# A four-part transformer kernel on one core: the order of all its jobs laid out anew, and the value products of two or three attention steps issued as one job

## The reference

```python
x = x + L0_attn(layernorm(x))      # one head, key and value width 64, causal, biases
x = x + L0_ffn(layernorm(x))       # fp8-quantized x @ weight.T + bias, 256 -> 256
x = x + L1_attn(layernorm(x))      # 16 heads of width 16, rotary embedding, causal
x = x + L1_ffn(layernorm(x))       # mixes with the row before, three 256x256 products

# L1_attn, the part that the change touches most
Q, K, V = (proj(W_Q), proj(W_K), proj(W_V))          # each [B, 16, S, 16]
Q = _apply_rope(Q, cos, sin); K = _apply_rope(K, cos, sin)
scores = jnp.einsum('bhsd,bhtd->bhst', Q, K) / jnp.sqrt(jnp.float32(D_K))
scores = jnp.where(causal[None, None], scores, -jnp.inf)
attn = jax.nn.softmax(scores, axis=-1)
out = jnp.einsum('bhst,bhtd->bhsd', attn, V)
out = out.transpose(0, 2, 1, 3).reshape(B, S, D_MODEL)
return jnp.einsum('bsd,ed->bse', out, W_O)
```

## Time and profile before

| what | value |
|---|---|
| median of 3 runs | 2517.73 us (2509.86 to 2520.37) |
| profiled execution, first to last instruction | 2514.1 us |
| PE / DVE / ACT / POOL busy | 2320.8 / 1985.3 / 1512.4 / 525.7 us |
| PE busy share | 92% |
| mean granted TensorE clock | 0.981 |

### The profile page before, as it was taken

One profiled execution on the slowest core, in us unless ns is written; L12 is line 12 of the kernel. 1 busy time (PEld: TensorE's weight loads), 2 busy tenths in 40 slices (PEclk: granted clock), 3 DMA queues, 4 the chain that ended last, 5 costly groups with the idle time before them and its releaser, 6 DMA issues.

```text
span 2514.1 us, 52353 instructions
## 1 busy us (share of the span) xinstructions
PE 2320.8 (92%) x19371; PEld 1053.0 (42%) x19371; DVE 1985.3 (79%) x4326; ACT 1512.4 (60%) x2753; POOL 525.7 (21%) x526
## 2 busy tenths in 40 slices
PE   8889899999999899998999999999999999999998
PEld 4544333333434335353444534344344434332345
DVE  5778689887787887879787787997788688899932
ACT  2234456575655666676675666657566577677762
POOL 5453210302215012120403303031121400000011
PEclk9899999999999999999999999999999999999999
DMA  2322220120211312021121302112021121110111
GB/s 56 83 72 73 76 58 25 38 59 18 83 34 35 82 43 73 15 79 29 42 65 37 91 19 76 40 35 78 12 76 35 42 70 45 31 42 27 28 37 36
DMA packets 185896, 125.41 MB, mean 50 GB/s; under 512 B 84912, under 2 KB 185392, under 8 KB 185648
## 3 DMA queue, kind: packets, MB, share of 16 engines
q1 hardware_dynamic: 184880, 121.16, 17.4%
q10 hardware_dynamic: 768, 0.92, 0.1%
HBM read 62.20 MB, written 59.24 MB: 48 GB/s over the span
## 4 chain that ended last, share of the span: by engine, by line
PE 55%; DVE 29%; ACT 6%; issue 4%; DMA 2%; SPq 2%; DVEq 1%; POOL 1%; POOLq 0%; ACTq 0%
DVE mx L1543 20%; PE psum L1867 12%; PE psum L1845 6%; PE psum L1812 6%; PE psum L1778 4%; ACT probs L1303 4%; PE psum L1742 3%; PE psum L1887 2%; PE psum L1713 2%; PE psum L1898 2%; PE psum L1651 2%; PE psum L1918 2%; PE psum L1799 2%; PE psum L1906 2%; DVE stats L1402 1%
## 5 line engine op out<-in xcount | busy, mean ns | idle before, releaser
L1303 ACT ACTIVATE probs<-psum 128x512 f32<-128x512 f32 x2176 | 1139.4, 607 | 465.8 <-PE psum L1845 310.2
L1543 DVE TENSOR_REDUCE mx<-psum 128x1 f32<-128x512 f32 (+2 forms) x2304 | 1283.4, 620 | 140.9 <-PE psum L1812 99.5
L1867 PE MATMUL psum<-probs,vs 128*17 128x512 f32 (+3 forms) x5120 | 590.7, 543 | 0.7 <-ACT probs L1303 0.3
L1812 PE MATMUL psum<-kst,qst 48*128 48x512 f16 (+3 forms) x2560 | 439.6, 354 | 71.0 <-DVE mx L1543 37.7
L1845 PE MATMUL psum<-qst,kst 50*128 50x512 f16 (+3 forms) x2560 | 428.7, 353 | 55.7 <-DVE mx L1543 19.5
L1812 PEld LDWEIGHTS psum<-kst,qst 48*128 48x128 f16 x2560 | 134.0, 94 | 397.5 <-DVE mx L1543 154.5
L1845 PEld LDWEIGHTS psum<-qst,kst 50*128 50x128 f16 x2560 | 128.2, 94 | 360.1 <-ACT probs L1303 131.4
L1867 PEld LDWEIGHTS psum<-probs,vs 128*17 128x17 f32 x5120 | 93.1, 96 | 155.5 <-issue 127.6
L1088 POOL TENSOR_SCALAR vare<-mv 128x4 f32<-128x4 f32 x64 | 15.5, 241 | 595.5 <-DVE mv L1405 595.5
L1819 PE MATMUL psum<-maskq,identh 64*128 64x128 bf16 (+1 forms) x2048 | 131.1, 205 | 0.0
L1117 POOL TENSOR_TENSOR sums<-probs 128x512 f32<-128x512 f32 x12 | 15.3, 1272 | 494.3 <-ACT probs L1257 494.3
(11 more groups left out here) (173 smaller groups left out, 2876.2 us busy)
## 6 DMA issues: line engine op xcount, KB each, us to landing
qk_dram<-parts SPq DMA_DIRECT2D x168, 128.0 KB
qst<-qk_dram SPq DMA_DIRECT2D x128, 96.0 KB, 2.3
kst<-qk_dram SPq DMA_DIRECT2D x128, 96.0 KB, 2.3
v_dram<-vst SPq DMA_DIRECT2D x64, 136.0 KB, 4.0
vs<-v_dram SPq DMA_DIRECT2D x64, 136.0 KB, 2.1
xs<-x_in SPq DMA_DIRECT2D x16, 512.0 KB, 3.5
x_dram<-xs SPq DMA_DIRECT2D x16, 512.0 KB, 2.9
att_dram<-ast SPq DMA_DIRECT2D x64, 128.0 KB, 2.0
```

The lines of the kernel that those rows point to most:

```text
L1303: act.activation(dst, src, ACT.Exp, scale=DK1 ** -0.5 / LIFT ** 2).then_inc(S["exp"], 1)
L1543: ins = dve.tensor_reduce(mx1[:, n % 2, 2 * g + odd, tile % TPC, c:c + 1], bank(src, at, at + cols), AX.X, ALU.max)
L1812: ins = pe.matmul(two[odd][:, at:at + cols], qst[rows, qslot, pair, P * (tile % TPC):P * (tile % TPC + 1)], kst[rows, kslot, pair, 0:cols] ...
L1867: ins = pe.matmul(bank(7, off, CH, rows=VW, row=32 * h), vtile[:, h, :], probs[:, HG * (step_no(b, hg, k) % PSTEPS) + h, at:at + CH - off] ...
```

## The change

Three things change; the arithmetic does not.

1. **`values` jobs.** Off the diagonal the products of two consecutive steps are one job, on the diagonal those of all three (`group_of`, `group_steps`). Such a job waits for all exponentials of its steps, and whoever waits for a step's values waits for the whole group's. There are 256 `values` jobs where there were 576, with the same 2560 matmuls of the program.
2. **The planner's numbers.** `HOP` is now one number per waiting engine and counts only between engines, `SWITCH` and several durations and landing times are other numbers, and a mode change that falls into a hole costs nothing.
3. **The planner's choice.** A stretch is 2.5 long instead of 40. What its rule is (how much staying in the mode counts, how much a pile of work before DVE or ACT holds back `max` and `scores`, and a weight for each kind on every engine) isn't tried out but drawn from a number in the table `RULES`, two characters a stretch.

Two `values` jobs have become one, and the `max` and `scores` jobs that stood between them stand on its two sides. The diff, cut to its core:

```diff
+def group_of(k):
+
+    q, kbs = STEPS[k]
+    return k - kbs[0] % 2 if kbs[0] < TPC * q else STEP_AT[q, TPC * q]
+
+
+def group_steps(k):
+
+    q, kbs = STEPS[k]
+    return range(k, k + 2) if kbs[0] < TPC * q else range(k, final_step(q) + 1)
+
+
+def valued(step):
+
+    return ("values", step and (*step[:2], group_of(step[2])))
...
-HOP = 0.25
-SWITCH = {("F", "R"): 0.31, ("F", "C"): 0.31, ("R", "F"): 0.15, ("R", "C"): 0.15, ("C", "F"): 0.14, ("C", "R"): 0.14,
...
-STICK = 100.0
+HOP = {"PE": 0.325, "DVE": 0.13, "ACT": 0.14, "POOL": 0.12, "SP": 0.1}
+SWITCH = {("F", "R"): 0.11, ("F", "C"): 0.10, ("R", "F"): 0.18, ("R", "C"): 0.10, ("C", "F"): 0.16, ("C", "R"): 0.08,
...
-STRETCH, WAYS, MOVE = 40.0, 8, 10.0
+STRETCH = 2.5
...
+        for at in range(len(RULES) // 2):
+            if state.todo:
+                rule = base * DIGITS.index(RULES[2 * at]) + DIGITS.index(RULES[2 * at + 1])
+                self.go(state, then, number, (at + 1) * STRETCH, self.rule(rule))
...
+    "!}!}!}!}!}!b%I!U,C!},U('$=*9!}!}!}!}!}!}!}!}!}!}!u+M!}!}$E!}!}!}!})^!u&j&r,A!n!e$1(n!u!I!(%Q$j$z"
...
+CAP = 3.0
+MOVES = (5.0, 20.0, 50.0, 120.0)
...
+    def rule(self, n):
+
+        if n == 0:
+            return 100.0, {"max": 50.0, "scores": 50.0}, {}
+        draw = np.random.RandomState(n)
+        share = draw.uniform(0, 1, 4)
+        move = MOVES[n % 4]
+        by = draw.uniform(-move, move, len(self.kinds))
+        return 150 * share[0], {"max": 100 * share[1], "scores": 100 * share[2]}, dict(zip(self.kinds, by))
...
+                load = {x: min(CAP, max(0.0, free_at[x] - now) + sum(jobs[name][2] for name in ready[x]))
+                        for x in ("DVE", "ACT", "POOL")} if e == "PE" else {}
...
-                    rank = (jobs[name][1] - (STICK if jobs[name][7] == mode and e == "PE" else 0.0) + weights.get(name[0], 0.0),
-                            number[name])
+                    rank = jobs[name][1] - (stick if jobs[name][7] == mode and e == "PE" else 0.0) + weights.get(name[0], 0.0)
+                    if e == "PE" and name[0] in press:
+                        rank += press[name[0]] * load[self.emptied[name[0]]]
+                    rank = (rank, number[name])
...
-                        ("scores", (b, hg, k, j)), ("values", two), lat=0.1, free=(("scores", (b, hg, k, j)), odd))
...
+                        ("scores", (b, hg, k, j)), valued(two), free=(("scores", (b, hg, k, j)), odd))
+            group += sum(CH - span(q, kb) for kb in kbs) / CH
+            if k == group_steps(group_of(k))[-1]:
+                n = group_of(k)
+                add("PE", "values", (b, hg, n), key + 5, 0.055 + 0.853 * group, *exps,
...
-                    wt.job("values", step_before(b, hg, k, PSTEPS))
+                    wt.job(*valued(step_before(b, hg, k, PSTEPS)))
...
-                    b, hg, k = item
-                    q, kbs = STEPS[k]
-                    for j in range(len(score_jobs(k))):
-                        for odd in range(2):
-                            wt.job("exp", (b, hg, k, j, odd))
-                    v_loaded(wt, b, hg, kbs[0] // TPC)
...
+                    b, hg, first = item
+                    for k in group_steps(first):
+                        q, kbs = STEPS[k]
+                        for j in range(len(score_jobs(k))):
+                            for odd in range(2):
+                                wt.job("exp", (b, hg, k, j, odd))
+                        v_loaded(wt, b, hg, kbs[0] // TPC)
```

More of the change, by code:

```diff
@@ L267, in run, with go @@
         state = State(left, self.listed, jobs)
[L268 to L281, removed]
+        self.kinds = sorted({name[0] for name in self.listed})
+        self.emptied = {}
+        for name in self.listed:
+            free = jobs[name][6]
+            if free:
+                self.emptied[(free[0] if free[0] in jobs else free)[0]] = jobs[name][0]
+        base = len(DIGITS)
+        for at in range(len(RULES) // 2):
+            if state.todo:
+                rule = base * DIGITS.index(RULES[2 * at]) + DIGITS.index(RULES[2 * at + 1])
+                self.go(state, then, number, (at + 1) * STRETCH, self.rule(rule))
+        assert not state.todo
         self.home, self.tenants, self.total, self.start = state.home, state.tenants, max(state.free_at.values()), state.start
         return state.order
[L285 to L293, removed]
+    def rule(self, n):
[6 more added lines that the diff above has]
+        return 150 * share[0], {"max": 100 * share[1], "scores": 100 * share[2]}, dict(zip(self.kinds, by))
+    def go(self, state, then, number, until, rule):
         jobs = self.jobs
@@ L353, in go @@
                 if e == "PE" and md != mode:
-                    time += SWITCH.get((mode, md), 0.0)
+                    time += max(0.0, SWITCH.get((mode, md), 0.0) - (now - free_at[e]))
                     mode = md
@@ L477, in chunk_jobs @@
         there = parts_before(b, q, bl)
-        add("PE", "RT", (*c, bl), key(), 0.43, ("RT", p and (*p, bl)), *[("roped", (*c, t)) for t in range(TPC)], ("put", there), lat=0.1,
+        add("PE", "RT", (*c, bl), key(), 0.43, ("RT", p and (*p, bl)), *[("roped", (*c, t)) for t in range(TPC)], ("put", there),
             claim="P", mode="F")
@@ L546, in head_jobs @@
         end = pos + UNIT * (q + 1)
-        add("ACT", "copy out", me, end - 20, 0.49, ("values", (b, hg, final_step(q))),
-            ("turnout", block_before(b, hg, q, 2)), free=("values", (b, hg, first_step(q))))
-        add("PE", "turnout", me, end + 2, 0.43, ("copy out", me), lat=0.1, claim="P", mode="F")
+        add("ACT", "copy out", me, end - 20, 0.49, valued((b, hg, final_step(q))),
+            ("turnout", block_before(b, hg, q, 2)), free=valued((b, hg, first_step(q))))
+        add("PE", "turnout", me, end + 2, 0.43, ("copy out", me), claim="P", mode="F")
@@ L573, in turn @@
     def turn(ln, source, *after):
-        add("PE", "turn", (ln, *c), key(), 0.87, source, lat=0.1, claim="D", mode="F")
-        add("ACT", "turned", (ln, *c), key(), 1.05, ("turn", (ln, *c)), *after, free=("turn", (ln, *c)))
+        add("PE", "turn", (ln, *c), key(), 0.873, source, claim="D", mode="F")
+        add("ACT", "turned", (ln, *c), key(), 0.92, ("turn", (ln, *c)), *after, free=("turn", (ln, *c)))
     def both(ln):
```

135 lines of the change are left out of this document (79 added, 56 removed).

## The result

The changed kernel takes 2403.74 us (median of 4 runs, 2395.5 to 2407.63) against 2518.61 of the kernel before (4 runs). The ratio is 0.9544, 95% interval 0.952 to 0.9568: 115 us faster, where 148 were forecast. Its profiled execution spans 2393.3 us, 120.8 less than before.

The account below looks back on a forecast made before the run. The bound was taken to be alternate starvation of PE and DVE. From 2514, 19 for mode changes and 130 for long runs came off, other terms 0, giving 2365, with 3.6 to the median told as 2370; whole range 2280 to 2470.

Parts of the forecast that it names:

- What bounds the kernel: Whole span: PE and DVE starve each other alternately; about 515 us of PE's time neither work nor mode change, 467 waits.
- Mode changes: PE's order: 1577 changes of array mode become 1387, at 0.10 us each, 19 us off.
- Long runs: PE stretches without `max` or `scores` starve DVE and ACT; shortening them saves 130 us, bounds 0 and 271.
- sum over 3.6: PE time beyond 3.6 us between two `max` jobs plus between two `scores` jobs: 310 + 359 before, 126 + 156 now.
- The burst: Grouped `values` hold PE 1.94 us, diagonal 2.37; DVE's waiting banks and ACT's idle time cover it, cost 0.
- Filling matmuls and the clock: Filling matmuls in plan holes fall from 311 to 204; cost 0, clock bounds -48 and +48 us.
- the fourth rival: The order doesn't do what it says: a falling clock shifts PE, slow stretches double (+48), 2505 us; no effect, 0.04.
- Head and tail: PE work before the first `max` goes from 57 to 62 us, after the last from 81 to 77; effect 0.
- the waits change hands: Rival: removed pauses come back as PE waiting on slower engines, a quarter of the 130 left, 2466 us; chance 0.24.
- three waits that I had named as signs: DVE's for `max` well under 99.5 us, ACT's for `scores` under 310.2, PE's weight loads for reductions no more than before.
- bursts starve DVE: Rival: at each of 256 `values` jobs DVE idles 0.74 us, 190 in all, giving 2559 or 2689 us; chance 0.05.

Follow-up runs that it names:

- e11: Changed kernel's planner with single-step `values` jobs and a rule table picked anew, keeping the 60 best plans: 2317.4 us, 0.9201 of the kernel before.
- e3: Changed kernel, `values` still grouped, with one fixed rule instead of the table and staying in the mode counting 0: 2615.8 us, 1.04 of the kernel before.
- e2: Changed kernel with one fixed rule instead of the table and each step's `values` a job of its own: 2511.5 us, 0.9979 of the kernel before.
- e1: Changed kernel, `values` still grouped, with one fixed rule for the whole plan instead of the table: 2630.2 us, 1.0463 of the kernel before.
- e5: Kernel before with grouped `values` jobs alone, keeping its own planner: 2653.7 us, 1.0537 of the kernel before.
- e9: As e3, but single `values` jobs free to stand apart, each still waiting for all exponentials of its group: 2616.4 us, 1.0395 of the kernel before.
- e6: As e1, but the ring of probabilities holds five steps instead of four: 2625.2 us, 1.0424 of the kernel before.
- e10: As e9, but each `values` job waits only for the exponentials of its own step: 2534.9 us, 1.0073 of the kernel before.
- e4: Changed kernel without any of its 204 filling matmuls: 2417.4 us, 0.9608 of the kernel before.

## Why the prediction was right or wrong

- *What bounds the kernel* held: PE and DVE starve each other in turn. DVE's work in the middle is 1901.6 us before, 1901.5 after and 1916.8 in e11, and the end follows how densely it stands: 82% before, 86.7% after (forecast 88, with 86 to 89 as the sign), 91% in e11.
- *Mode changes*, 19 us: 14 in PE's account, which counts those at filling matmuls too. A merged pair takes 1.84 to the next job, as said: 2104.71 to 2106.56 in the rows above, and 1.844 is the median over all 192 two-step jobs.
- *Long runs*, 130 us: the sign and the place were right, the reasoning of its size was not. DVE's idle time under F jobs fell by 120 us. But the measure "sum over 3.6" doesn't tell the time: e3 has 345 and takes 2616, e2 has 599 and takes 2512. What the table of rules buys is not evenness by that measure, and it is worth 226 us on grouped jobs. That it does so by setting each job where its banks and operands are ready is argued, not shown by a run.
- *The burst* is the step that failed. It was put at 0 because DVE's stock covers 1.94 us and ACT's wait for the ring is idle anyway. In fact grouping costs 119 us with one rule (e1 and e2) and 134 in the kernel before (e5). The prediction priced PE's burst and the ring, and neither is the net cost (e9, e6); it mentioned that a group waits for all its exponentials and priced nothing for it, and that wait is worth 82 us (e9 and e10). So the forecast's 19 + 130 - 0 = 149 us stand against 7 for the planner's numbers with one rule, 226 for the table and -119 for grouping, 115 together: a larger gain and a cost that I had left out stood against each other. That the time came out 34 us from the forecast and inside its range is in good part luck. The kernel's own planner could have shown the cost beforehand: with one rule, its plans with and without groups end 111 us apart.
- *Filling matmuls and the clock* were put at 0: e4 has all 204 fillings at 14 us; what the 107 fewer of the change did by themselves no run shows. The clock rose from 0.981 to 0.989 with 107 fewer of them, so the direction of the fourth rival is out too.
- *Head and tail* at 0: the last 100 us are as they were, DVE 27.46 after and 26.66 in the same stretch before.
- The rival *the waits change hands* is partly there. Of the three waits that I had named as signs, two were to fall well under 99.5 and 310.2 and came to 90 and 305; the third, weight loads for reductions, was to be no more than before and fell from 154.5 to 129. The first two were bad signs: DVE's time came from its waits for projections, such as the 2.16 in the earlier trace rows. Its waits for `QK1`, `V0`, `WO1` and `V` together fell from 156 to 65 us, the one for `max` by 10. The rival *bursts starve DVE* had the side right for the part alone: with grouping and nothing else the kernel is slower than before. e5 at 2654 even lies in that rival's 2559 to 2689. Its mechanism, the burst, is there but pays for itself (e9).

## What to carry to other kernels

Small jobs that need no shared buffer are what an in-order engine fills its waits with; joining them into larger ones, each waiting for all its inputs, saved 0.1 us a piece here and cost more than it saved. When a change has two parts, run each alone: this one is the sum of a part worth -7 - 226 us and one worth +119, and a kernel without the second, with rules picked for it, is 86 us faster. A count over an order (run lengths, changes of mode) says where to look, and ranks orders only after it has been tried on two or three of them. Where the order comes from a simulation, read first what that simulation says of each part of the change.

## What the runs showed of the hardware

- A change of the array's mode shows as 0.09 to 0.12 us between starts. Between e3 and e9, 391 more of them, 415 with those at filling matmuls, took 41 to 56 us of PE's account, by how the undisturbed times are told: 0.10 to 0.14 each. The Trainium skill, "TensorEngine Tiling (Array Packing)", Key Properties, says that such a change drains the array; the traces agree, and give it that price.
- With the 204 filling matmuls taken away (e4) the mean granted clock went from 0.989 to 0.972, with 139 us at the lower of its two levels instead of 53, and the time rose by 14 us, a third of what the clock alone would give.
